# Normalised rows lowered and transposed one token tile at a time, with two transfers for a pair of tiles

## What is computed

```python
x = x + xattn0(layernorm(x), ctx, mask)    # 16 heads of 32, 77 keys, masked
x = x + ffn0(layernorm(x))                 # rows quantised to 8 bits, ternary weights
x = x + xattn1(layernorm(x), ctx)          # 16 heads of 64, 77 keys, output projection
x = x + ffn1(layernorm(x))                 # Fourier-domain weights, folded into one 512x512 matrix
```

## Time and profile before

| | us |
|---|---|
| median of 3 runs | 1085.54 (1085.15 to 1088.56) |
| profiled execution | 1083.82 |
| its span, first to last instruction | 1082.0 |

### The profile page before, as it was taken

How to read it: one execution, slowest core, us unless ns; L and a number is a source line. 1 busy time by engine, 2 the same in 40 slices (tenths; PEclk the granted TensorE clock), 3 DMA queues, 4 the chain that set the end, 5 groups by cost and what they waited for, 6 DMA issues and landing times.

```text
span 1082.0 us, 18058 instructions
## 1 busy us (share of the span) xinstructions
PE 906.5 (84%) x6236; PEld 501.7 (46%) x6236; DVE 815.7 (75%) x1435; ACT 669.2 (62%) x1936; POOL 568.8 (53%) x584
## 2 busy tenths in 40 slices
PE   1868888686869989997998799889978996897884
PEld 0537764343435544554554455444544554344431
DVE  7977766578997789778977887888789778636632
ACT  2526954285786787677767884877687767307401
POOL 2306656144483577466736665585468456614404
PEclk9989989897989999999999999999999997898796
DMA  9742582867666556748585767666576734613603
GB/s 284 147 132 47 124 148 67 181 125 201 114 109 131 105 111 115 179 80 147 89 193 91 128 127 147 117 116 143 125 118 114 168 74 88 134 28 59 107 30 78
DMA packets 352475, 130.42 MB, mean 121 GB/s; under 512 B 333439, under 2 KB 342592, under 8 KB 349439
## 3 DMA queue, kind: packets, MB, share of 16 engines
q1 hardware_dynamic: 352383, 129.25, 58.4%
HBM read 33.57 MB, written 15.96 MB: 46 GB/s over the span
## 4 chain that ended last, share of the span: by engine, by line
PE 49%; DVE 18%; ACT 10%; DMA 8%; POOL 6%; issue 5%; SPq 3%; ACTq 0%; POOLq 0%; DVEq 0%
PE wb L188 14%; PE wb L189 13%; PE wb L190 13%; ACT pr L919 5%; PE wb L1463 3%; DMA prT<-ph 3%; DMA xT<-xh 3%; DVE xh L1188 3%; ACT xh L944 2%; DVE parts L999 2%; DVE ph L1270 2%; POOL pr L766 2%; SPq L572 1%; PE scores L188 1%; PE scores L190 1%
## 5 line engine op out<-in xcount | busy, mean ns | idle before, releaser
L766 POOL TENSOR_TENSOR pr<-pr,sm 128x616 f32<-128x616 f32 x128 | 175.3, 1370 | 266.8 <-DVE sm L1265 266.2
L919 ACT ACTIVATE pr<-scores,bound,factor 128x77 f32<-128x77 f32 x640 | 255.6, 419 | 8.6 <-ACT bound L913 0.8
L188 PE MATMUL wb<-xT,wq_hl 128*128 128x512 f16 (+1 forms) x400 | 151.9, 380 | 22.4 <-DMA xT<-xh 18.3
L189 PE MATMUL wb<-xT,wq_hl 128*128 128x512 f16 (+1 forms) x400 | 152.0, 380 | 0.0
L190 PE MATMUL wb<-xT,wq_hl 128*128 128x512 f16 (+1 forms) x400 | 151.5, 379 | 0.0
L919 ACT ACTIVATION_READ_ACCUMULATOR pr<-scores,bound,factor 128x1 f32 x640 | 132.6, 207 | 0.0
L932 ACT ACTIVATE ph<-pr 128x618 f16<-128x618 f32 x128 | 93.2, 729 | 61.7 <-POOL pr L766 31.2
L188 PE MATMUL wb<-wo_hl,qc 128*128 128x512 f16 x276 | 104.6, 379 | 5.5 <-DVE qc L1195 4.1
L190 PE MATMUL wb<-wo_hl,qc 128*128 128x512 f16 x276 | 104.6, 379 | 0.0
L189 PE MATMUL wb<-wo_hl,qc 128*128 128x512 f16 x276 | 104.6, 379 | 0.0
L754 POOL TENSOR_SCALAR rstd<-moments 128x2 f32<-128x2 f32 (+1 forms) x48 | 13.9, 290 | 160.2 <-DVE moments L1159 159.0
(11 more groups left out here) (215 smaller groups left out, 2440.1 us busy)
## 6 DMA issues: line engine op xcount, KB each, us to landing
xr<-in_x SPq DMA_DIRECT2D x6, 1024.0 KB, 5.9
out_x<-xr SPq DMA_DIRECT2D x6, 1024.0 KB, 4.9
xr<-in_wk SPq DMA_DIRECT2D x3, 1024.0 KB, 7.1
xr<-in_wq SPq DMA_DIRECT2D x3, 1024.0 KB, 10.1
xr<-in_wv SPq DMA_DIRECT2D x3, 1024.0 KB, 6.5
k1b<-scr_k SPq DMA_DIRECT2D x16, 154.0 KB, 5.3
scr_k<-k1b SPq DMA_DIRECT2D x7, 308.0 KB, 7.0
x<-in_x SPq DMA_DIRECT2D x2, 1024.0 KB, 7.2
```

Source lines behind the costliest of these rows:

```text
L188: pe.matmul(out, lhs(0), rhs(0), start=start, stop=False, **kw)
L189: pe.matmul(out, lhs(0), rhs(1), start=False, stop=False, **kw)
L766: pool.tensor_tensor(v, v, s, ALU.mult).then_inc(probs_ready, 1)
L919: ins = act.activation(pr[U % 3][:, h // 4, cols], sc[:, U % 2, h // 4, cols], ACT.Exp, bias=bound[:, U % 2, h:h + 1], scale=k["factor"][: ...
```

## The change

The low half is made by two instructions, one for each tile, the first with a semaphore of its own (`first_lowered`), the second with the old one (`ln_lowered`). SP issues two transposes of half the size, the second behind a wait for the second tile. For the quantised rows the computation is unchanged, and only the transfer is cut in two. A pair's transfers now count 32 on their semaphore, and all who wait for them wait for both.

```diff
+LOWERED = {e: n for n, e in enumerate([e for e in APPLIED if e[0] != 1])}
...
         def rows_of(j, pair, b):
             n = APPLIED[j, pair, b]
-            return rows_turned[n % 2], 16 * (n // 2 + 1)
+            return rows_turned[n % 2], 32 * (n // 2 + 1)
...
             def turn_rows(j, pair, b):
                 n = APPLIED[j, pair, b]
-                sp.wait_ge(ln_lowered, n + 1)
+                sp.wait_ge(*((ln_lowered, n + 1) if j == 1 else (first_lowered, LOWERED[j, pair, b] + 1)))
...
-                if j == 1:
-                    o, i = qiT[:, pair:pair + 2, :, :].rearrange("p t c n -> p (t c) n"), quantised(n).rearrange("p t d -> p (t d)")
-                else:
-                    o = (xT4 if j == 3 else xT)[:, pair:pair + 2, :, :, :].rearrange("p t h c n -> p (t h c) n")
-                    i = xh[:, n % 2, :, :, :].rearrange("p t h d -> p (t h d)")
-                sp.dma_start_transpose(o, i).then_inc(rows_turned[n % 2], 16)
+                for t in range(2):
+                    if j == 1:
+                        o, i = qiT[:, pair + t, :, :], quantised(n)[:, t, :]
+                    else:
+                        if t == 1:
+                            sp.wait_ge(ln_lowered, n + 1)
+                        o = (xT4 if j == 3 else xT)[:, pair + t, :, :, :].rearrange("p h c n -> p (h c) n")
+                        i = xh[:, n % 2, t, :, :].rearrange("p h d -> p (h d)")
+                    sp.dma_start_transpose(o, i).then_inc(rows_turned[n % 2], 16)
...
-                    act.wait_ge(rows_turned[n % 2], 16 * (n // 2))
+                    act.wait_ge(rows_turned[n % 2], 32 * (n // 2))
...
-                dve.tensor_tensor(xh[:, n % 2, :, 1, :], xn[:, :, :], xh[:, n % 2, :, 0, :], ALU.subtract).then_inc(ln_lowered, 1)
+                dve.tensor_tensor(xh[:, n % 2, 0, 1, :], xn[:, 0, :], xh[:, n % 2, 0, 0, :], ALU.subtract).then_inc(first_lowered, 1)
+                dve.tensor_tensor(xh[:, n % 2, 1, 1, :], xn[:, 1, :], xh[:, n % 2, 1, 0, :], ALU.subtract).then_inc(ln_lowered, 1)
```

More of the change, by code:

```diff
@@ L327, in layers @@
         keys_cleared, values_cleared = sem("keys_cleared"), sem("values_cleared")
-        vb1_in, zeroed, pool_idle, eye_in = sem("vb1_in"), sem("zeroed"), sem("pool_idle"), sem("eye_in")
+        vb1_in, zeroed, pool_idle, eye_in, first_lowered = sem("vb1_in"), sem("zeroed"), sem("pool_idle"), sem("eye_in"), sem("first_lowered")
         nsin_in, fold_ready, fold_hi, fold_lo = sem("nsin_in"), sem("fold_ready"), sem("fold_hi"), sem("fold_lo")
@@ L1167, in quantise @@
                 if n >= 2:
-                    dve.wait_ge(rows_turned[n % 2], 16 * (n // 2))
+                    dve.wait_ge(rows_turned[n % 2], 32 * (n // 2))
                 step(dve.tensor_reduce(amax[:, pair], xn[:, :, :], AX.X, ALU.max, apply_absolute_value=True))
```

## The result

The changed kernel takes 1097.06 us (median of 4 runs, 1096.63 to 1101.31), the kernel before in the same sessions 1086.57 (1085.15 to 1088.56). The ratio is 1.0104 with a 95% interval of 1.0073 to 1.0135: 11.3 us slower (7.9 to 14.7), where 12.5 were forecast. The profiled execution is the longest of the four: 1101.31 us, span 1099.5, at a mean granted clock of 0.935, where the others had 0.941 to 0.944 and the profiled execution of before 0.947. So part of what the two traces show between them (17.5 us of span) belongs to that execution and not to the change.

The account below looks back on a forecast made before the run. TensorE, busy 84%, was taken to bound most of a pass, with three stretches of waits holding the changed rows. The terms 4.8 + 0.5 + 6.0 + 0.6 + 0.4 + 0.2 gave 12.5 us, so 1098 us, range 1086 to 1104.

Parts of the forecast that it names:

- the pair (0,2): Lowering at 688.38 us: GpSimd runs between the halves, delaying ScalarE's exponentials in four passes, 4 x 1.2 = 4.8 us.
- the transfers: Row transfers on SP: +0.1 us a pass near 692 us, zero for quantised pairs.
- (2,0): Lowering at 724.65 us: GpSimd between the halves delays the landing at 738; 6.0 us in five passes, 0.6 in the first.
- rival 4: Pair (3,0) at 678.66 us: GpSimd comes between the halves there too, 6 us more, 1104 us; chance 0.10.
- Rival 1: VectorE's two halves: nothing comes between them anywhere, 1.5 us in all, 1087 us; chance 0.14.
- the exponentials start 1.3 - 0.1 us later: ScalarE after pair (0,2): GpSimd's later low half delays the exponentials, with 0.1 us of slack; 4.8 us in four passes.
- later against TensorE by 1.2 us: Sign of being right in the profile after: ScalarE's exponentials behind the lowering of (0,2) come 1.2 us later against TensorE.
- the -0.45: Near 680 us: prT, queued on SP behind a pair, lands 0.45 us earlier; counted as 0 in the sum.
- the +0.1: Near 692 us: four half transfers issued in a row land 0.1 us later than two whole ones; counted as 0.
- the slower line (d): VectorE and GpSimd line through the pair (0,2) at 688.38 us to ScalarE's exponentials, taken to set the pace there.
- Rival 2: Only one of the delays at (0,2) and (2,0) reaches the end: about half, 6 us, 1091.5 us; chance 0.13.
- The halves elsewhere, 0.06 us each: Two undisturbed 128x512 lowerings take 1.28 us against 1.22 for one of 128x1024: 0.06 us added per pair.

Follow-up runs that it names:

- +2.0: Kernel before with only the transfers of pairs (0,0) and (0,2) cut in two: 1087.67 us, +2.0 us, ratio 1.0018.
- +6.4: Kernel before with the transfers of all pairs other than (0,0) and (0,2) cut in two: 1091.40 us, +6.4 us, ratio 1.0059.
- the +3.1: Kernel before with only the 16 transfers of quantised rows cut in two: 1089.75 us, +3.1 us, ratio 1.0029.

## Why the prediction was right, and where its steps were wrong

**The total: partly luck.** 12.5 us were forecast and 11.3 measured. One term of the sum is 4.8 us too high (the pair (0,2), which costs nothing), and the transfers, put at 0.1 us a pass or at zero, are too low, in the change by up to some 4 us. The path and the size of the largest term, (2,0), were right.

**The mechanism: right.** A waiting instruction of GpSimd runs between two adjacent ones of VectorE, and the second half ends 1.14 us later (forecast 1.3). It does so at (0,2), at (2,0) and at the end, and not at (3,0), where it misses by 0.05 us: rival 4 was as near as it was said to be. Rival 1 is excluded by every pass. (Its price was also added up wrong: 0.06 x 5 and up to 0.1 is 0.3 to 0.4 us a pass, 1.8 to 2.4 us in six, not 1.5.) The SBUF - State Buffer page of the Trainium skill, Who interferes with whom, says that issue order decides who blocks; the rows at (2,0) and (3,0) agree, with 0.04 us after the first half's start on the one side and 0.05 after the second's on the other.

**(2,0), 6.6 us: right in size and nearly in place.** +7.6 alone, and 7.3 inside the change, there with its transfer. TensorE meets the delay not ahead of the 103x512 products (L1463), where the sign of being right was put, but a little earlier, ahead of the scores (L1430), a wait that its row puts down to ScalarE's exponentials. It is 0.88 us a pass where 1.2 were taken (1.15 in one), and nothing in the first pass: 4.7 us in the trace, the rest not located.

**(0,2), 4.8 us: wrong, it costs nothing.** The step that failed is "the exponentials start 1.3 - 0.1 us later". Under it lies a misread condition: the low half that ends at 699.06 was taken for the one of the unit three before, and it is that of the unit two before; the right one had ended 2.5 us earlier. So there were 2.5 us of slack, not 0.1. In the kernel with (0,2) alone in two the exponentials start 0.65 us ahead of TensorE's product of xT, before 0.62: the sign "later against TensorE by 1.2 us" did not come. The line that sets the pace near 700 us is TensorE leaving xT, SP's row of transfers, their landing, and (0,2) is not on it; that also undoes the reason for which the -0.45 and the +0.1 of the transfers were set aside as lying "beside the slower line (d)". Rival 2 (only one of the two reaches the end) was the true case for the lowerings in its outcome, with 0.13 of the chances, though not for the reason it gave.

**The transfers, 0.1 to 0.2 us: wrong.** By themselves they cost 11.7 us (6.3 to 17.2). In the change, with (2,0) left whole, 4.0 us stay (2.2 to 6.0) for the other transfers and the other lowerings. The traces speak for the transfers: in that kernel the waits for `qc` and xT together are 3.84 to 4.70 us in the five passes, 3.2 us more in all than before, and with the lowerings alone in two the pair of waits hardly grew. One part of the term was mis-sized: the row of four lands 0.5 us later than the two (7.38 against 6.86), where the sum had 0.1. The fourth is issued 4.03 us after the first where 3 x 1.27 = 3.81 were taken, and it lands 3.35 us after its issue instead of 3.1. A quantised pair holds SP for 2.50 us in two issues where one took 1.23, the upper end of the range given. The rest of this term was not in the sum at all: more stretches run at the lower level, of which I had said "1 to 2 us, both ways". It went one way, by about 8 us between the two traces, a part of which is the two executions and not the change. The Trainium skill's page DMA: Bandwidth & Descriptors, Rules for kernel authors, advises to coalesce transfers, and I had priced it at under 1 us. Its row speaks of sizes under 64 KB, and the pieces here are of 256 and 128 KB; the runs agree with its direction, at +11.7 us for 64 transfers cut in two.

**The halves elsewhere, 0.06 us each: right in size.** 1.28 to 1.30 us where undisturbed; at (3,2) 2.26 or 2.27 against 2.20 before.

**The first tile sooner, -0.45 us, hidden: right in kind.** The landing of prT gains 0.26 us at TensorE near 686 us, and most of it is hidden in the wait that follows. The end: +0.1 forecast, and TensorE's last wait went from 11.45 to 11.38 us. With the lowerings alone it was 12.59, and with the transfers alone 11.59: the delay of the lowering there is made up by the second transfer, which lands 3.1 us after its issue instead of 4.3, as worked out.

**The parts do not add.** +9.5 and +11.7 alone give 11.3 together. The rows show a part of the reason. The sum of the wait for `qc` and the wait for xT near 490 us is 3.55 us before, 3.70 with the lowerings in two (and a new one of 0.72 right behind), 4.15 with the transfers in two, 4.08 with both; and for prT at 480 us it is 1.01, 1.08, 1.30 and 0.75, as only with both is the first tile really sent sooner. Against the transfers alone that is 0.55 us in this pass. The rest is open. That the broken-up wait (2.25 + 1.83 against 0.45 + 3.70) also keeps the clock up is only argued; behind it the granted clock was 1.00 in one pass and 0.50 in another.

**Open.** The transfers' parts (+2.0 and +6.4) give 8.4 against 11.7 for the whole, within the intervals. Of the +6.4 and the +3.1 no wait was found that explains them; the clock was seen to be lower, but what share of it is the transfers' and what the execution's own was not settled.

## What to carry to other kernels

Cutting an instruction in two on an engine that shares SBUF access opens a door: look up what the neighbour has waiting at that moment, and price the gap at one whole instruction of the neighbour. Then follow the delay to the next wait on the bounding engine, and ask whether what that wait is for starts from the delayed line or from something else; only in the first case does it cost. Where a chain of waits puts one instruction behind another whose end happens to fit to 0.01 us, look up in the program which count of the semaphore is needed and which instruction brings it, and test by delaying that instruction: here the chain named one that was no condition at all.

## What the runs showed of the hardware

- The order in which GpSimd and VectorE reach SBUF is decided at every instruction. GpSimd's addition that came 0.04 us after the first half's start ran ahead of the second half (2.37 us for the two halves); its low half that came 0.05 us after the second half's start had to wait (1.82 us for what takes 1.32), and the two halves took 1.30. Making the neighbour wait only shifted the delay to VectorE's next instruction that collides (0.17 us became 1.09).
- A DMA transpose of half the size (128x1024 fp16) holds SP for 1.23 us, or 1.32 when it directly follows another, and lands after 3.1 to 3.4 us; one of a quarter (128x512) for 1.19 or 1.26, and lands after 2.5. Whole: 1.93 and 4.7. So a cut in two costs SP 0.6 us and more for a whole one, and 1.2 us for one of half the size, as the smaller one is hardly faster to issue.
- TensorE's clock in the stretch right behind its wait for xT, over six passes in each of the fourteen traces: below full speed (0.50 to 0.70) behind 26 of the 28 waits of 3.36 to 4.13 us, and behind 20 of the 56 shorter ones. So a longer wait goes with the lower level, but its length alone does not settle it (1.00 behind 3.80 and 3.90 us in two traces, 0.50 behind 0.84 in a third). A stretch at the lower level costs 1.2 to 2.8 us. Executions of the kernel before spread by 7.6 to 11.7 us within a session, more than most of the differences looked for here; the longer ones tend to have the lower clock, which does not show which of the two is the cause.
